# Feed-forward expert weights split once in an earlier stage, kept in DRAM, and read through a ring of three halves that TensorE addresses by a register

## The reference, cut to what matters

```
last   = y[:, -1, :]                          # the last token of each batch
logits = gelu(last @ Wp1 + bp1) @ Wp2 + bp2
sel    = argmax(softmax(logits))              # one of 8 experts for each batch
z      = gelu(y @ W1[sel] + b1[sel]) @ W2[sel] + b2[sel]   # W1 512x1024, W2 1024x512
x1     = x + z @ Wo + bo
```

## Time and profile before

| | us |
|---|---|
| median of three runs | 2916.85 |
| lowest and highest run | 2916.61, 2922.43 |
| span of the profiled execution | 2914.5 |
| PE busy | 2574.8 (88%) |
| DVE busy | 1479.1 (51%) |
| ACT busy | 1200.6 (41%) |
| POOL busy | 724.8 (25%) |
| splits of the feed-forward weights, ACT (L1041) | 256.6, 256 of them |
| splits of the feed-forward weights, DVE (L1083) | 354.1, 256 of them |
| read from and written to DRAM | 425.67 MB and 77.76 MB |

### The profile page before, as it was taken

One profiled execution on the slowest core, in us unless ns is written; L12 is line 12 of the kernel. 1 busy time (PEld: TensorE's weight loads), 2 busy tenths in 40 slices (PEclk: granted clock), 3 DMA queues, 4 the chain that ended last, 5 costly groups with the idle time before them and its releaser, 6 DMA issues. The chain is left out here.

```text
span 2914.5 us, 41950 instructions
## 1 busy us (share of the span) xinstructions
PE 2574.8 (88%) x12487; PEld 2061.8 (71%) x12487; DVE 1479.1 (51%) x1826; ACT 1200.6 (41%) x1773; POOL 724.8 (25%) x604
## 2 busy tenths in 40 slices
PE   6999999977787568888888886699997999999999
PEld 1788888866666456666666664599996888888876
DVE  4311111146666577777777774477664233333346
ACT  3111111146676455555555552466664222222223
POOL 0222222021222146555555554000000111111100
PEclk9999999989899889999999998799998999999999
DMA  6222222034634253335333531566664111111125
GB/s 246 33 63 51 51 51 43 14 120 121 195 109 130 88 172 121 123 122 177 118 122 120 176 121 65 205 231 224 232 237 163 37 29 33 33 29 29 29 76 169
DMA packets 136778, 328.58 MB, mean 113 GB/s; under 512 B 41762, under 2 KB 44258, under 8 KB 129056
## 3 DMA queue, kind: packets, MB, share of 16 engines
q1 hardware_dynamic: 113744, 258.70, 27.1%
q0 software_dynamic: 22992, 69.37, 8.1%
HBM read 425.67 MB, written 77.76 MB: 173 GB/s over the span
## 5 line engine op out<-in xcount | busy, mean ns | idle before, releaser
L1083 DVE TENSOR_TENSOR s_w_lo<-s_w_raw,s_w_hi 128x1024 fp32r<-128x1024 f32 x256 | 354.1, 1421 | 3.0 <-ACT s_w_hi L1041 3.0
L1041 ACT ACTIVATE s_w_hi<-s_w_raw 128x1024 fp32r<-128x1024 f32 x256 | 256.6, 1052 | 103.8 <-PE s_z_ps L88 72.3
L395 DVE TENSOR_TENSOR s_h<-s_sg,s_up 128x512 f32<-128x512 f32 x64 | 43.9, 687 | 395.7 <-ACT s_sg L290 395.6
L86 PE MATMUL s_g<-wx_hi,s_x_hi 128*128 128x512 f32 x512 | 206.7, 404 | 6.5 <-DVE s_x_lo L1604 4.0
L88 PE MATMUL s_g<-wx_hi,s_x_lo 128*128 128x512 f32 x512 | 201.8, 394 | 0.0
L87 PE MATMUL s_g<-wx_lo,s_x_hi 128*128 128x512 f32 x512 | 201.1, 393 | 0.0
L607 POOL DMA_INDIRECT s_x<-in_x_rows,s_idx x72 | 92.4, 1284 | 405.5 <-DMA s_idx<-mid_slot_token 387.0
L1338 DVE TENSOR_TENSOR s_w_lo<-s_w_raw,s_w_hi 128x1024 fp32r<-128x1024 f32 x128 | 150.9, 1221 | 68.1 <-ACT s_w_hi L1290 66.4
L290 ACT ACTIVATE s_sg<-s_gate 128x512 f32<-128x512 f32 x64 | 38.3, 599 | 291.2 <-PE s_up L88 291.2
L86 PE MATMUL s_z_ps<-s_w_hi,s_ht_hi 128*128 128x512 f32 x256 | 110.6, 432 | 50.8 <-DVE s_ht_lo L1099 47.4
L1505 POOL DMA_INDIRECT s_y<-mid_hash_out,s_rec x32 | 31.5, 985 | 488.2 <-DMA s_rec<-mid_rec 488.2
(11 more groups left out here) (305 smaller groups left out, 7296.8 us busy)
## 6 DMA issues: line engine op xcount, KB each, us to landing
s_w_raw<-in_rw SPq DMA_DIRECT2D x144, 512.0 KB
s_w_raw<-in_w SPq DMA_DIRECT2D x32, 2048.0 KB
s_w_raw<-in_w SPq DMA_DIRECT2D x64, 1024.0 KB
s_w_raw<-in_w1h SPq DMA_DIRECT2D x16, 2048.0 KB, 8.2
s_w_raw<-in_w2h SPq DMA_DIRECT2D x16, 2048.0 KB, 7.7
mid_routed<-s_o_sb SPq DMA_DIRECT2D x72, 256.0 KB, 3.1
s_b<-in_b SPq DMA_DIRECT2D x32, 512.0 KB
s_x_grp<-in_xt_groups POOLq DMA_DIRECT2D x8, 1024.0 KB, 5.7
```

The source lines that it names most:

```text
L86: pe.matmul(out, a_hi, w_hi, start=first, stop=False, skip_group_check=True)
L1041: act.activation(hi[:, c], raw[:, c], ACT.Copy).then_inc(S[name + "_hi"], 1)
L1083: dve.tensor_tensor(lo[:, c], raw[:, c], hi[:, c], ALU.subtract).then_inc(S[name + "_lo"], 1)
```

## The change

1. **Split once.** In the shared stage the 8 experts' W1 and W2 are split, one expert for each of the 8 token groups, in 8 parts of 512 KB. For each part SP loads it (`raw_part`), ACT makes the high part (`part_hi`), DVE the low one (`part_lo`), and SP stores both, 1 MB (`store_part`), to a DRAM tensor `mid_w` of 67 MB. There are two buffers for it. They are taken from `x_grp[:, 1]` and from four working tables (`pool_b`) that the stage needs only at its start, so the first part waits for `rec_done`. Parts 0 to 5 stand between the chunks of a group on ACT and DVE, parts 6 and 7 beside the down product.
2. **Tables.** The choose stage computes on DVE, beside the old table, the rank of each batch's expert (7 - expert), the ring's slot for its W1 and W2, and how many batches come before each expert's end: 21 small instructions more on the serial chain, and two less.
3. **The ring.** In the feed-forward stage `half` holds three *halves*; a half is W1 or W2 of one expert, high and low, 4.19 MB. SP does nothing else than load all 16 halves in order, expert 7 first, chosen or not. Half h goes to slot h mod 3; from the fourth on it first waits until the last batch that uses half h-3 is done with it (`h_ps`, `mm2`). It then waits for its own landing before it looks at the next. TensorE loads rank and slots of a batch into registers (`look_up`), waits for `half_in` (half 2\*rank before `up`, half 2\*rank+1 before `down`) and addresses the weights through the register.
4. **The other DMAs.** Every other load and store of the stage moves from SP's queue to ACT's, 11 a batch with 7 value loads, between ACT's own pieces. The lags on ACT grow by one. The copy of 127 partitions into `prev` becomes two, of 112 and 15. The splits of the weights on ACT and DVE are gone from the stage.

The core of the diff:

```diff
+            def part_step(g, j):
+                if isinstance(g, int) and g == 0 and j == 0:
+                    sp.wait_ge(S["w_lo"], NU)
+                    raw_part(0, 0)
+                    raw_part(0, 1)
+                    return
+                sp.wait_ge(S["part_lo"], g * NPART + j)
+                store_part(*((g, j - 1) if j else (g - 1, NPART - 1)))
...
+                for j in range(PART_EARLY):
+                    part_step(g, j)
+                store_o(g, 0)
+                part_step(g, PART_EARLY)
...
+                act.activation(part[j % 2][:, 0].bitcast(FP32R), w_raw[:, j % 2], ACT.Copy).then_inc(S["part_hi"], 1)
...
-            software_pipeline(sp, NB, [(2, load_b2), (1, load_w1), (5, store_r), (0, load_rec), (0, load_params),
-                                       (1, load_w2(0)), (1, load_b1), (3, store_x1), (0, load_x), (1, load_w2(1))])
+            for h in range(2 * ER):
+                if h >= NW:
+                    used = (h - NW) // 2
+                    batches = sp.value_load(table[0:1, 0, NB + used:NB + used + 1], min_val=0, max_val=NB)
+                    if (h - NW) % 2 == 0:
+                        sp.wait_ge(S["h_ps"], batches * 2 + 1)
+                    else:
+                        sp.wait_ge(S["mm2"], batches + 1)
+                    sp.nop(nofuse=True)
+                sp.dma_start(half[:, h % NW].bitcast(FP32), d["w"][2 * (ER - 1 - h // 2) + h % 2]).then_inc(S["half_in"], 16)
+                sp.wait_ge(S["half_in"], 16 * h + 16)
...
-                sp.dma_start(prev[1:P], x1[0:P - 1]).then_inc(S["prev_in"], 16)
+                for p0, p1 in ((0, 112), (112, P - 1)):
+                    act.dma_start(prev[p0 + 1:p1 + 1], x1[p0:p1]).then_inc(S["prev_in"], 16)
...
             software_pipeline(act, NB, [
-                (1, w2(0, 2)), (4, copy_r), (1, gelu(0)), (2, part_hi(z_hi, tz_ps, "tz", "mmo", "z_hi")), (1, gelu(1)),
-                (1, h_hi(0)), (1, w2(2, 3)), (1, h_hi(1)), (3, part_hi(xr_hi, tz_ps, "txr", "mmr", "xr_hi")),
-                (1, w2(3, 4)), (0, w1(0, 2)), (0, part_hi(y_hi, ty_ps, "ty", "h_ps", "y_hi")), (0, w1(2, 4))])
+                (0, load_params), (5, copy_r), (2, gelu(0)), (3, part_hi(z_hi, tz_ps, "tz", "mmo", "z_hi")), (2, load_b2), (2, gelu(1)),
+                (2, h_hi(0)), (2, h_hi(1)), (1, load_b1), (4, part_hi(xr_hi, tz_ps, "txr", "mmr", "xr_hi")), (5, store_r),
+                (0, load_rec), (0, load_x), (3, store_x1), (1, part_hi(y_hi, ty_ps, "ty", "h_ps", "y_hi")),
+                (3, load_hrec)])
...
+            def look_up(i):
+                now["rank"] = order_of(pe, 2, i, ER - 1)
+                for n in range(2):
+                    now[f"slot{n + 1}"] = pe.value_load(table[0:1, n, bass.ds(i, 1)], min_val=0, max_val=NW - 1)
+
             def up(n):
                 def stage(i):
                     if n == 0:
                         pe.wait_ge(S["y_lo"], i + 1)
+                        pe.wait_ge(S["half_in"], now["rank"] * 32 + 16)
```

More of the change, by code:

```diff
@@ L31 @@
 DVE_BIG = 3.0e38
+NW = 3
 def wait_for(eng, sem, n):
@@ L119, in stage_shared @@
     NU = 12
+    d["w"] = nc.dram_tensor("mid_w", [2 * ER, P, 2, DC, HS], FP32, kind="Internal").ap()
     with ExitStack() as ctx:
@@ L854, in stage_ffn @@
         ps = lambda n, s, t=FP32: ctx.enter_context(nc.psum_tensor("s4_" + n, s, t))
-        S = sems(nc, ctx, "s4_", "params_in rec_in hrec_in shared_in x_in ~routed1_in ~routed2_in b1_in b2_in w1_in "
-                 "w2_in0 w2_in1 w1_hi w1_lo w2_hi w2_lo part_y y base x_plus_y bo_scaled ty y_hi y_lo h_ps h_add gelu th h_hi "
+        S = sems(nc, ctx, "s4_", "params_in rec_in hrec_in shared_in x_in ~routed1_in ~routed2_in b1_in b2_in half_in "
+                 "part_y y base x_plus_y bo_scaled ty y_hi y_lo h_ps h_add gelu th h_hi "
                  "h_lo mm2 z_add tz z_hi z_lo mmo x1 x1_out prev_in dx k_part xk r_part xr ~xk_sent txr xr_hi "
@@ L1031, in _, with load_rec @@
         def _(act):
-            def split_w(name, raw, hi, mm, per, c0, c1):
-                def stage(i):
-                    if name == "w2":
-                        act.wait_ge(S[f"w2_in{c0 // 2}"], i * 16 + 16)
-                    elif c0 == 0:
-                        act.wait_ge(S["w1_in"], i * 16 + 16)
-                    if c0 == 0:
-                        wait_for(act, S[mm], i * per)
-                    for c in range(c0, c1):
-                        act.activation(hi[:, c], raw[:, c], ACT.Copy).then_inc(S[name + "_hi"], 1)
-                return stage
+            def load_rec(i):
+                b = order_of(act, 1, i, NB - 1)
+                wait_for(act, S["y"], i)
+                act.dma_start(rec[:], d["rec"][b]).then_inc(S["rec_in"], 16)
+                act.dma_start(shared[:], d["shared"][b]).then_inc(S["shared_in"], 16)
@@ new lines, in load_x, with load_params @@
+            def load_x(i):
+                b = order_of(act, 1, i, NB - 1)
+                wait_apart(act, S["base"], i)
+                act.dma_start(x[:], ins["x_rows"].rearrange("(b p) n -> b p n", p=P)[b]).then_inc(S["x_in"], 16)
+            def load_params(i):
+                if isinstance(i, int) and i == 0:
+                    for dst, src in ((bo, "bo"), (maa_k, "maa_k"), (maa_r, "maa_r")):
+                        act.dma_start(dst[:], ins[src].partition_broadcast(P)).then_inc(S["params_in"], 16)
@@ L1134, in combine, with weights @@
                                          ALU.mult, ALU.add).then_inc(S["y"], 1)
[L1136 to L1137 removed]
             software_pipeline(dve, NB, [
[L1139 to L1142 removed]
+                (2, h_add(0)), (1, combine), (3, part_lo(z_lo, tz_ps, z_hi, "z_hi", "z_lo")), (2, h_add(1)),
+                (2, h_lo(0)), (3, x1_), (2, h_lo(1)),
+                (4, part_lo(xr_lo, tz_ps, xr_hi, "xr_hi", "xr_lo")), (1, part_lo(y_lo, ty_ps, y_hi, "y_hi", "y_lo")),
+                (2, z_add)])
         @block.tensor
         def _(pe):
+            now = {}
+            def weights(slot, part, k, c0, c1):
+                return half[:, bass.ds(slot, 1), part, k, c0:c1].rearrange("p o n -> p (o n)")
+            def look_up(i):
+                now["rank"] = order_of(pe, 2, i, ER - 1)
+                for n in range(2):
+                    now[f"slot{n + 1}"] = pe.value_load(table[0:1, n, bass.ds(i, 1)], min_val=0, max_val=NW - 1)
             def up(n):
```

234 lines of the change are left out of this document (124 added, 110 removed).

## The result

The changed kernel takes 3315.45 us, median of five runs (3289.83 to 3324.59), against 2916.85: 1.135 times as long, 95% interval 1.1325 to 1.1378. The forecast was 3062 with a range to 3120. The direction was right; the loss is 2.7 times the one forecast. In seven profiles of kernels with this shared stage the next stage begins anywhere from 707 to 729 us, so part of that difference arises there; the rest stays open.

The account below looks back on a forecast made before the run. It took the copy loop into prev, 24 us a batch, as the bound, replaced by ACT's queue at 26.0. Terms 4 + 4 + 52 + 64 + 50 - 24 = +150 gave 3067, taken as 3062 us, range 2965 to 3120.

Parts of the forecast that it names:

- the copy's loop: Feed-forward stage before: the 16 us copy into prev, then dx to xk and x1, sets 24 us a batch.
- lie inside those 24 us: Feed-forward stage before: weight splits, 8 x 1.05 us on ACT and 8 x 1.42 on DVE a batch, hidden in the copy's loop.
- Cost nothing, while the parts come in time: Shared stage: 64 parts' splits, 67 us on ACT and 91 on DVE, fit beside PE; the stage gets +4 us.
- The bound of +40: Shared stage: upper bound of its term, if POOL's list chain gets late past 612 us.
- The same price if the parts come later than a chunk: Shared stage: within the rival of a longer stage, late parts also cost +46 us, 3108 us; rival's chance 0.15.
- Choose, start, switches, end: Choose stage, feed-forward start, expert switches and feed-forward end: +4, +52, +50 and -24 us.
- The 11.6 us by the fit of the Trainium skill: Weight loads: a half by 2.0 us plus bytes over 436 GB/s, 25 us less in the sum; not used.
- Period, 26.0 forecast: Feed-forward stage: ACT's queue sets T = 26.0 us a batch (24.5 to 28), +64 us over 31 intervals.
- the 26.7: Feed-forward stage: links from one up(0) to the next in ACT's order total 26.7 us, taken as 26.0 for overlap.
- ACT's sequencer goes on past a waiting instruction: Feed-forward stage: rival in which DMA issues run ahead and PE's 18.5 us bounds the loop, 2888 us; chance 0.10.
- The rival in which the loop bounds in part: Feed-forward stage: ACT blocks but the records' chain overlaps the gelus, T 22.5 to 24, 2955 to 3010 us; chance 0.20.
- register-addressed weights cost PE: Feed-forward matmuls: rival in which register addressing costs PE, at 1.5 us a batch +48, 3110 us; chance 0.05.

Follow-up runs that it names:

- e9_prev127: e8_best with the copy into prev as one of 127 partitions again: 2997.39 us in one run, +146, batches every 23.7 us.
- e1_prev: The kernel before with only the copy into prev made in two pieces, of 112 and 15: 2897.87 us, ratio 0.9938 to before.
- e13_warm_longer: The change with 37 matmuls of no use on PE ahead of the wait for y_lo: 3261.37 us, ratio 1.1185 to before.
- e8_best: The change with feed-forward DMAs on SP, halves loaded only for a new expert, last in SP's step, and shared-stage parts spread: 2851.53 us, ratio 0.9775 to before.
- e12_warm_pe: The change with 24 matmuls of no use on PE ahead of the wait for y_lo: 3303.00 us.
- e4_prev127: The change with the copy into prev as one of 127 partitions again, on ACT's queue: 3441.36 us in one run, 126 more than the change.

## Why the prediction was wrong, point by point

- **What bounds before.** Right that the copy's loop is 24 us (e9_prev127), but incomplete: it said that the splits "lie inside those 24 us", and didn't ask what DVE and POOL do once they meet. Before, POOL waited for the copy while DVE split; in e1_prev they met, and the batch stayed at 23.9 us.
- **Shared stage, +4 forecast, +96 measured. The step that failed** is "Cost nothing, while the parts come in time", with its comparison of 193 + 45 GB/s to the 351 of the earlier trace rows. 351 is the rate of a short window of large loads; loads and stores beside POOL's lists came to 185 to 211 GB/s with the engines 0.83 to 0.92 busy. And an average rate was the wrong thing to compare: the cover is one chunk of 5.6 us for a load and a store, 1.57 MB, which by the prediction's own price (1.8 us and 350 GB/s) already take 6.3; the loads took 11.1. The bound of +40 was taken from the wrong mechanism: not POOL's chain got late (it was done at 587 in the changed profile instead of some 480, still 120 us ahead of the stage's end), but ACT waited for part loads, and silu behind it. The rival "The same price if the parts come later than a chunk" had the place, but 45 us for it.
- **Choose, start, switches, end.** +3.7, +49.3, +52.4, -19.6 against 4, 52, 50 and -24. A half landed in 13.5 us (12.3 to 15.4), one every 13.9 at the start, where 14.1 with its issue was taken; the start moved 353 GB/s. The row's 350 GB/s was right. The 11.6 us by the fit of the Trainium skill ("DMA: Bandwidth & Descriptors", Anatomy of one DMA) were too short; the page states that fit for DMAs issued by GpSimd, and the halves are issued by SP.
- **Period, 26.0 forecast, 30.5 measured. The mechanism was right, the size was off.** All links are in the trace. Four sizes: `up(0)` to the second `h_hi` took 12.5 instead of 10.0, since the sum took PE's pace from the earlier trace rows although its 26.0, with 18.5 of work for PE, left PE idle 7.5 us in each batch; 2.3 of it is the 12 matmuls at 0.427 (e13_warm_longer gives back 2.0). The records took 3.5 to reach POOL instead of 2.1. And the four issues of `store_x1` with `load_x` took 4.2 to `y_hi`, where 3.3 was taken. The links add up without overlap, so taking 0.7 us off the 26.7 for the seams was wrong too. POOL's gather and base were 1.3 shorter than taken.
- **Rivals.** That ACT's sequencer goes on past a waiting instruction fell, for both kinds of instruction. A DMA issue that waits holds what stands behind it: `y_hi` stood behind `load_x`, and moving it alone gave 153 us. A compute instruction that waits holds the sequencer too: the second `h_hi` of 1343.37 waited 1.83 us for PE, and the sequencer's next instruction started 7 ns after it did; in all 32 batches it is 5 to 7 ns. The earlier trace rows alone didn't show this, since there a register operation at 1318.38, ahead of the gelu, was what waited. The Trainium skill ("Perfetto Trace Analysis", DVE / Act Engine Instruction) has the sequencer free once the instruction is pushed into a wait queue; the trace doesn't agree with it. That register-addressed weights cost PE fell as well: `e8_best` runs at 18.8 a batch with them. The rival in which the loop bounds in part was priced at 2955 to 3010; its own terms, added up, give 2972 to 3018.

## What to carry to other kernels

ACT's and SP's queues here were each one line: a DMA with a wait, put between an engine's own pieces, delayed all that stood behind it, even a load that moved nothing, so the piece that starts the next round must stand ahead of it. When transfers are to hide behind other work, compare the landing of each with the time from its issue to its use, and not the bytes of the whole stage with the best window of loads; and take the landing from a stretch with the same mix of reads, writes and small transfers. And if a forecast says that PE will idle for many us in each round, as for 8.7 here, price its next matmuls at the lower clock.

## What the runs showed of the hardware

- DVE and POOL stretched each other where both read two operands from SBUF: the same split took 1.21 us alone and 2.31 beside POOL, POOL's operations 1.3 and 2.16 (e1_prev). The Trainium skill ("SBUF — State Buffer", SBUF: two separate sides) says that the two share a port pair as a lock in this case. The rows agree in that both get longer, and only where they overlap; whether it is a lock or a shared rate they don't tell.
- After 8.7 us of idle time (the change), and also after 3.1 (e12_warm_pe), PE's matmuls started 0.427 apart at a granted clock of 0.50, the level of 1.2 GHz; with the idle time filled (e13_warm_longer) they started 0.23 apart, and the kernel with more work was faster.
- While the second `h_hi` of a batch waited for its semaphore, mostly for 1.83 us, ACT's sequencer did nothing: in all 32 batches of the change its next instruction started 5 to 7 ns after this `h_hi` did. Behind the copy of 127 partitions the next DMA issue took 3.6 us on ACT's queue (e4_prev127) and 5.8 on SP's (median, before).
- Large loads moved 351 to 353 GB/s with the DMA engines 0.88 to 0.94 busy; large loads and stores beside POOL's chain of small transfers 185 to 211 with 0.83 to 0.92, and the same without the chain 207 with 0.62. What in the chain costs the engines so much was not taken apart.
